# Writing out the last lap of an edge join and routing each 16 tiles inside it

## The reference, cut to what matters

```python
h = (x_flat @ W_gat).reshape(M, HEADS, NUM_EXPERTS)         # 4 heads, 4 experts
e = leaky_relu(a_src[src] + a_dst[dst], 0.2)                # each edge and head
ee = exp(e - segment_max(e, dst)[dst])
alpha = ee / (segment_sum(ee, dst)[dst] + 1e-16)
agg = segment_sum(h[src] * alpha[:, :, None], dst) + b_gat
scores = layernorm(agg, ln_gamma, ln_beta).reshape(M, HEADS, NUM_EXPERTS).mean(1)
topk_s, topk_i = top_k(scores, 2); w = softmax(topk_s)
out = sum over experts of gate * (gelu(x @ W1[e] + b1[e]) @ W2[e] + b2[e])
```

## Time and profile before

| what | us |
| --- | --- |
| median of 3 runs | 1663.26 (1662.75 to 1664.58) |
| profiled execution | 1661.68 |
| its span | 1659.9 |
| DVE busy | 1253.1 |
| PE busy | 873.8 |
| POOL busy | 868.6 |
| ACT busy | 444.9 |

### The profile page before, as it was taken

How to read it: one execution, slowest core, us unless ns; L and a number is a source line. 1 busy time by engine, 2 the same in 40 slices (tenths; PEclk the granted TensorE clock), 3 DMA queues, 4 the chain that set the end, 5 groups by cost and what they waited for, 6 DMA issues and landing times. The chain is left out here.

```text
span 1659.9 us, 37280 instructions
## 1 busy us (share of the span) xinstructions
PE 873.8 (53%) x13446; PEld 687.8 (41%) x13446; DVE 1253.1 (75%) x2683; ACT 444.9 (27%) x801; POOL 868.6 (52%) x892
## 2 busy tenths in 40 slices
PE   0232333268888825544888836656666556544300
PEld 0222233157777725542333325555555545444300
DVE  6989988866666647978999966677667667555599
ACT  0222222134444425751333312111111111111100
POOL 0045654646666630003777777760777777777200
PEclk9555555556767656765999965555555555555555
DMA  7000000122222234003110011100111111101001
GB/s 166 0 21 23 28 26 21 52 46 49 51 51 48 58 48 97 4 24 35 11 10 10 10 10 12 12 11 4 12 12 13 12 13 14 12 12 11 6 10 40
DMA packets 114003, 45.95 MB, mean 28 GB/s; under 512 B 92647, under 2 KB 108831, under 8 KB 113586
## 3 DMA queue, kind: packets, MB, share of 16 engines
q1 hardware_dynamic: 84098, 22.43, 7.1%
q0 software_dynamic: 27680, 19.22, 6.8%
q10 hardware_dynamic: 2064, 2.10, 0.6%
HBM read 28.26 MB, written 15.93 MB: 27 GB/s over the span
## 5 line engine op out<-in xcount | busy, mean ns | idle before, releaser
L335 POOL DMA_INDIRECT edges_rows<-table,edges_src x576 | 552.7, 960 | 175.6 <-issue 175.6
L191 DVE TENSOR_TENSOR sorting_keys<-sorting_keys 128x512 f32<-128x512 f32 (+2 forms) x370 | 209.7, 608 | 17.0 <-ACT sorting_keys L316 13.7
L727 POOL DMA_INDIRECT y_rows<-mixture_yt,mixture_xin x144 | 157.1, 1091 | 103.5 <-ACT mixture_yt L949 79.6
L722 POOL DMA_INDIRECT x_rows<-mixture_sent,mixture_slot x128 | 144.4, 1128 | 127.3 <-DVE mixture_slot L784 88.8
L2348 ACT ACTIVATE edges_hotT<-edges_h 128x1024 bf16<-128x1024 bf16 x74 | 71.7, 1021 | 391.4 <-PE edges_h L2247 391.4
L1062 PE MATMUL mixture_bank<-mixture_xT,sorting_w_part 128*128 128x128 bf16 x864 | 109.6, 254 | 32.4 <-ACT mixture_xT L935 17.2
L1062 PEld LDWEIGHTS mixture_bank<-mixture_xT,sorting_w_part 128*128 x864 | 85.3, 105 | 58.4 <-issue 46.4
L1897 DVE TENSOR_TENSOR edges_work<-edges_feats,all_eo 128x2048 bf16<-128x2048 f32 x48 | 109.3, 2277 | 0.2 <-DVE all_eo L1950 0.2
L2247 PE MATMUL edges_h<-edges_ident,edges_work 128*128 128x128 bf16 x592 | 68.7, 308 | 32.7 <-DVE edges_work L1897 32.7
L1897 DVE TENSOR_TENSOR edges_work<-edges_feats,edges_local 128x2048 bf16<-128x2048 f32 x37 | 84.4, 2282 | 0.3 <-DVE edges_stray_src L2053 0.3
L2301 PE MATMUL edges_acc<-edges_term_parts,edges_work 128*128 128x20 bf16 x1728 | 51.8, 179 | 60.5 <-DVE edges_term_parts L1776 60.5
(11 more groups left out here) (477 smaller groups left out, 2168.0 us busy)
## 6 DMA issues: line engine op xcount, KB each, us to landing
edges_rows<-table,edges_src POOLq DMA_INDIRECT x576, 2.4
mixture_xin<-x_rows SPq DMA_DIRECT2D x144, 49.0 KB, 1.8
all_eo<-y_rows SPq DMA_DIRECT2D x16, 256.0 KB, 3.9
y_rows<-mixture_yt,mixture_xin POOLq DMA_INDIRECT x144, 2.6
sorting_w<-in_L_ffn_w_dram SPq DMA_DIRECT2D x4, 512.0 KB, 8.4
x_rows<-mixture_sent,mixture_slot POOLq DMA_INDIRECT x128, 2.3
out_dram<-all_x_sb SPq DMA_DIRECT2D x8, 256.0 KB, 2.6
constants_src_i<-in_L_ffn_edge_index_dram SPq DMA_DIRECT2D x1, 1024.0 KB, 5.0
```

Of the source, the lines that this page charges most:

```text
L191: self.st.mark(dve.tensor_tensor(target[half], source[0], source[1], (ALU.min, ALU.max)[half]))
L335: pool.indirect_dma_start(to, None, rows, where).then_inc(done, 16)
L722: pool.indirect_dma_start(x_rows, bass.IndirectOffsetOnAxis(ap=slot[g % 2][:, c, t:t + 1], axis=0), now[c][:, t, :], None).then_inc(scatte ...
L727: pool.indirect_dma_start(y_rows, bass.IndirectOffsetOnAxis(ap=xin[j % XB][:, ROWX - 2:ROWX - 1].bitcast(U32), axis=0), yt[j % YB][:, :], ...
```

## The change

Four things are done together.
- **The last lap is written out** on every engine, and only the laps between the first and the last are a hardware loop (for this data one). In the last lap the order is group-major (`group_major`): the three turns of group 0, then those of group 1, and so on. POOL gathers in that order too. The floor of turns becomes seven.
- **Routing moves into the last lap.** When a group's three turns are done, its 16 tiles are routed during the three steps of the next group: `route_gaps` behind the first fetch of sums, `route_totals`, `route_scores` and `route_image` ahead of the wait for `now` in the first, second and third step, and the second half of the image work at the third step's end. The last group is routed behind the last step. The reduction over experts becomes two additions. The block `route` goes; its buffers are carved from the spent `stacks`, and its small loads are issued in `graph`. The mask `absent` is made ahead of the strays.
- **Keys are fetched further on**: POOL issues the key gather behind the last group of the second turn. DVE places sources of turns 0 and 1 in the 7th step of a lap, and those of turn 2 in the 9th, where it first waits for all gathers of the third turn. The last lap fetches no keys.
- **Fields, flags and the fetch of sums** are handled by lap: local numbers and flags of three turns are placed at once at a lap's end, and each step but a lap's first fetches the sums of the step before, also across turns. The last step of the last lap makes no next one-hots.

```diff
-        st.link(dve.tensor_scalar(self.most[:, :], self.most[:, :], float(LAP + 1), float(LAP - 1), ALU.max, ALU.add))
+        st.link(dve.tensor_scalar(self.most[:, :], self.most[:, :], float(2 * LAP + 1), float(LAP - 1), ALU.max, ALU.add))
-        st.link(dve.tensor_copy(self.laps[:, 0:1], self.thirds[:, :]))
+        st.link(dve.tensor_scalar(self.laps[:, 0:1], self.thirds[:, :], 1.0, None, ALU.subtract))
...
+        def turn_major(s):
+            return s // GROUPS % LAP, s % GROUPS
+
+        def group_major(s):
+            return s % LAP, s // LAP
...
-                        if u == 1 and g == 0 and not first:
-                            wait_apart(pool, at_ready, lap + 2, spare)
-                            gather(pool, krow[:, :], key_elements, at_i[0:T, :], keys_in)
+            for s in range(SEQ):
+                gather_group(0, *turn_major(s))
+            with pool.Fori(1, last_lap) as lap:
+                for s in range(SEQ):
+                    u, g = turn_major(s)
+                    gather_group(lap, u, g)
+                    if u == 1 and g == LAST:
+                        wait_apart(pool, at_ready, lap + 2, spare)
+                        gather(pool, krow[:, :], key_elements, at_i[0:T, :], keys_in)
+            for s in range(SEQ):
+                gather_group(last_lap, *group_major(s))
...
             dve.tensor_copy(times[:, :], times_ps).then_inc(times_read, 1)
+            dve.wait_ge(times_read, 1)
+            st.mark(dve.tensor_scalar(absent[:, :], times[:, :], 0.0, NONE, ALU.is_le, ALU.mult))
...
+            def route_gaps(q):
...
+                now = tiles(q)
+                rt.link(dve.tensor_tensor(shared, last_row[:, Q:ROW].unsqueeze(1).to_broadcast([P, TP, HEADS]), ad_sb[:, now, :], ALU.add))
+                rt.link(dve.scalar_tensor_tensor(shared, shared, 0.2, shared, ALU.mult, ALU.max))
+                rt.link(dve.tensor_tensor(shared, shared, per_channel(absent[:, now], HEADS), ALU.add))
+                rt.link(dve.tensor_tensor(top, tops[:, now, :], shared, ALU.max))
+                rt.mark(dve.tensor_tensor(gaps[:, 0, :, :], tops[:, now, :], top, ALU.subtract))
+                gaps_marks[q] = rt.n
+                dve.tensor_tensor(gaps[:, 1, :, :], shared, top, ALU.subtract).then_inc(gaps_ready, 1)
+
+            def route_totals(q):
...
+                dve.wait_ge(exps_ready, q + 1)
+                rt.mark(dve.tensor_tensor(by_head(total), by_head(sums[:, now, :]), wide(exps[:, 0, :, :], NE + 1), ALU.mult))
...
+                rt.link(dve.tensor_tensor(agg, agg, vector(0), ALU.add))
+                norm.center(dve, rt, agg, agg)
+
+            def route_scores(q):
...
+                norm.scale(dve, rt, agg, q, normed)
+                dve.wait_ge(normed, q + 1)
...
+                rank = order.unsqueeze(1).to_broadcast([P, TP, NE])
+                for n, values in enumerate((scores, others)):
+                    rt.link(dve.tensor_reduce(firsts[n], values, X, ALU.max))
+                    rt.link(dve.tensor_tensor(chosen, values, per_channel(firsts[n], NE), ALU.is_equal))
+                    rt.link(dve.tensor_tensor(chosen, chosen, rank, ALU.mult))
+                    rt.link(dve.tensor_reduce(best, chosen, X, ALU.max))
+                    rt.link(dve.tensor_tensor(masks[n], rank, per_channel(best, NE), ALU.is_equal))
...
+            def route_image(q, half=0):
...
+                rt.link(dve.tensor_tensor(weighted, eo[:, now, :].rearrange("p t (e c) -> p t e c", e=K),
+                                          gate[:, half * TB:(half + 1) * TB, :].unsqueeze(3).to_broadcast([P, TB, K, C]), ALU.mult))
+                rt.link(dve.tensor_tensor(added2, weighted[:, :, 0:2, :], weighted[:, :, 2:4, :], ALU.add))
+                rt.link(dve.tensor_tensor(x_sb[:, now, :], x_sb[:, now, :], added2[:, :, 0, :], ALU.add))
+                dve.tensor_tensor(x_sb[:, now, :], x_sb[:, now, :], added2[:, :, 1, :], ALU.add).then_inc(result, 1)
+                dve.wait_ge(result, b + 1)
+
+            def join_lap(lap, st, order_of, first=False, final=False):
...
-                        if g > 0:
-                            add_sums(u, g - 1)
...
+                        if s > 0:
+                            add_sums(s - 1)
+                        if final and s >= LAP and s % LAP == 0:
+                            route_gaps(done)
+                        if not first and not final:
+                            if s == GROUPS + LAST - 1:
+                                dve.wait_ge(keys_turned, lap + 2)
+                                place_sources(st, 0)
+                                place_sources(st, 1)
+                            if s == 2 * GROUPS:
+                                for n in range(GROUPS):
+                                    dve.wait_ge(rows_in[2][n], lap * (16 * GB) + 16 * GB)
+                                place_sources(st, 2)
+                        if first and s == SEQ - 1:
                             place_sources(st, 2)
-                            dve.wait_ge(flags_ready, lap * LAP + LAP)
+                        if s == SEQ - 1 and not final:
+                            dve.wait_ge(flags_ready, lap + 1)
                             keep_fields(st)
-                        if g == LAST:
-                            place_fields(st, (u + 1) % LAP)
+                            place_fields(st)
...
-                        one_hot(nxt)
+                        if not final or s < SEQ - 1:
+                            one_hot(s + 1, *order_of((s + 1) % SEQ))
...
                         st.mark(dve.tensor_copy(old, now[:, :]))
-                        dve.wait_ge(now_ready, at(u, g))
+                        if final and s >= LAP:
+                            (route_totals, route_scores, route_image)[s % LAP](done)
+                        dve.wait_ge(now_ready, at(s))
...
-                        if g == LAST:
-                            add_sums(u, g)
...
+                        if final and s >= LAP and s % LAP == LAP - 1:
+                            route_image(done, 1)
+                        if s == SEQ - 1:
+                            add_sums(s)
...
+            join_lap(last_lap, Steps(dve, final_steps), group_major, final=True)
+            route_gaps(GROUPS - 1)
+            route_totals(GROUPS - 1)
+            route_scores(GROUPS - 1)
+            route_image(GROUPS - 1)
+            route_image(GROUPS - 1, 1)
...
+            for s in range(SEQ):
+                done = s // LAP - 1
+                if done >= 0:
+                    if s % LAP == 0:
+                        route_exps(done)
+                    elif s % LAP == 1:
+                        norm.scalar(act, done)
+                    else:
+                        route_gate(done)
+                exp_group(turns * GROUPS + s, s, s < SEQ - 1)
```

More of the change, by code:

```diff
@@ L1 @@
 import itertools
+import math
 from contextlib import ExitStack
@@ L1640, in graph, with take @@
                               for n in range(2))
+        spent = [v[:, :].bitcast(F32) for v in stacks]
+        weighted = spent[0][:, 0:TB * K * C].rearrange("p (t e c) -> p t e c", t=TB, e=K)
+        added2 = spent[0][:, TB * K * C:TB * K * C + TB * 2 * C].rearrange("p (t e c) -> p t e c", t=TB, e=2)
+        vec = a.sb("vec", [P, 3, F])
+        last_row = a.sb("last_row", [P, ROW])
+        absent = a.sb("absent", [P, T])
+        used = 0
+        def take(*shape):
+            nonlocal used
+            words = math.prod(shape)
+            used += words
+            v = spent[1][:, used - words:used]
+            if len(shape) == 1:
+                return v
+            names = "abc"[:len(shape)]
+            return v.rearrange(f"p ({' '.join(names)}) -> p {' '.join(names)}", **dict(zip(names, shape)))
+        shared, top = take(TP, HEADS), take(TP, HEADS)
+        gaps, exps = take(2, TP, HEADS), take(2, TP, HEADS)
+        part3, total, inverse = take(TP, Q), take(TP, Q), take(TP, HEADS)
+        agg, scores, gate = take(TP, F), take(TP, NE), take(TP, NE)
+        order, chosen, others = take(NE), take(TP, NE), take(TP, NE)
+        best, gap2, gap2_exp = take(TP), take(TP), take(TP)
+        masks, firsts = [take(TP, NE) for _ in range(2)], [take(TP) for _ in range(2)]
+        shares = [take(TP) for _ in range(2)]
+        norm = Norm(a, "norm", TP, F, 1e-5, take(TP, F))
         carved = 0
```

360 lines of the change are left out of this document (161 added, 199 removed).

## The result

| | before | after |
|---|---|---|
| median (range) of the runs, us | 1663.44 (1662.75 to 1664.58) | 1599.07 (1597.70 to 1600.27) |
| span of the profiled execution, us | 1659.9 | 1598.4 |
| after / before | | 0.9612 [0.9595, 0.9629] |

The changed kernel is 3.9% faster; 1601 was forecast. Names of buffers and lines have moved with the change: the step's first instruction is L2219 now, the fetch of sums L2211, the gathers L336, the matmuls of `now` L2449, the routing pieces L2138 to L2199.

What follows compares the result with a forecast made beforehand. The prediction saw VectorE's chain of 36 steps, POOL's gathers beside it and a serial VectorE tail as bounds. 1513.1 + 56.0 + 28.8 = 1597.9 us of span, 62.0 less, so a median of 1601; range 1590 to 1617 (0.80).

Steps and rivals of the forecast that it cites:

- Key gather: On POOL, moved three groups later: reached at 1176.4 us with 21 us of margin, where 43.6 us of wait stood.
- POOL's end: POOL's gather stream: 19 groups of 20.07 us and one key gather after 1116.2, ending at 1498.8 us, against 1546.8.
- Start of the join: VectorE's first join step: 997.14 us plus 0.4 for the absent mask moved ahead of it.
- Laps 1 and 2: VectorE's first two laps of the join: 170.8 us, ending at 1168.3, then 175.5 us, ending at 1343.8.
- The term of the boundary: Fetching sums at each turn's end on VectorE: 2.3 us per boundary inside a lap, removed except at a lap's end.
- Last lap without routing: VectorE's written-out third lap: 13.1 + 10 x 14.1 + 15.2, together 169.3 us, ending at 1513.1.
- Routing in the lap: Three quarters on VectorE, 24.5 us each less 5.7 of cover in waits for PE: 56.0 us added.
- ScalarE: Six function table loads of 1.28 us in the last lap, costed at nothing; 7.7 us if not covered.
- (b): Rival: keys still come late, the 9th step of lap 2 waits 22 us for rows, 1623 us; chance 0.03.
- (a): Rival: routing in the lap is not covered; 17 us more gives 1618, up to 1628; chance 0.07 beyond 1617.
- (c): Rival: instruction fetch stalls the written-out last lap, slower than before, 1696 us with two refetches a step; chance 0.03.
- (d): Rival: the join does not shorten, late rows only change places with routing, 1653 us; chance 0.02.

Runs made afterwards that it cites:

- one-hot ahead: Version with both waits covered and the mask moved, plus 4 of 16 tiles of the next one-hot made before the fetch of sums; 1584.18 us, ratio 0.9537.

## Why the prediction was right, point by point

- **Key gather.** Near 1176 without a wait; it was at 1180.14. The move has its cause and price confirmed from both sides.
- **POOL's end.** Forecast 1498.8, measured 1514.5, the largest miss of a point. POOL reached the key gather 3.7 us late. The 256 gathers behind it take 333.1 us (1181.38 to 1514.51), 20.8 a group and not 20.07: they are 1.00 us long in the mean, four of them stretched by 7.1 us together (last section), while POOL waits for nothing but its own issue. The 20.07 was low by the earlier trace rows too, whose 552.7 and 175.6 us over 576 gathers make 20.23. It cost nothing with routing in the lap. But the forecast also held that POOL would be in time "even with no routing in the lap", and that was wrong: there the last gather was issued at 1505.45 and the last step came 6 us late. The forecast had set POOL's end against the end of the last step (1513.1), while a step wants its rows at its start, which by the same terms was 1497.9 and ahead of POOL's 1498.8.
- **Start of the join.** 1001.46, not 997.5. Of the 3.9, 2.2 already stand where `graph` loads its first constants, behind stages whose code is the same (748.18 became 750.34). The rest was counted as 0.4, and isn't split here. Part of it is spread between executions: two more traces with the code of the kernel before up to this point start the join at 998.62 and 998.84, where the earlier trace rows has 997.14.
- **Laps 1 and 2.** 172.2 and 175.1 us, where 170.8 and 175.5 were forecast. A plain step took 14.03, not the 13.93 of the earlier trace rows. The steps that place sources are 0.8 and 1.0 longer (1242.85, 1257.64, 1272.70), 0.6 was counted. **The term of the boundary was right in size and wrong in kind**: 2.3 is 1.3 of fetch and 1.0 of placing, and the placing wasn't removed but gathered at the lap's end, where the last step grew from 18.02 to 18.69.
- **The loop's end.** 3.94 us of idle time became 0.39. The kernel before with the moved keys still shows 3.51 there.
- **Last lap without routing.** 169.3 forecast; 13.0 + 10 x 14.03 + 14.34 = 167.6 by the trace with all routing behind it. The last step was the mis-sized term, 15.2 against 14.34; the plain steps, 14.1 against 14.03, add 0.7.
- **Routing in the lap.** 56.0 forecast, 54.1 measured. A quarter by itself is 24.98 with its 0.9 of waits for ScalarE, which the forecast counted apart: 24.05 without them against 24.5. The cover was 6.9 a quarter, 0.9 of it these waits and 6.0 the waits for TensorE, where 5.7 was counted. So the pieces were a little shorter and the cover a little wider than forecast. The place of the cover was right: the list of waits lost nine waits for `now`, and the piece behind the term's parts took the three at the sums.
- **Tail.** 28.8 forecast, 27.9 measured (1570.48 to 1598.4).
- **ScalarE.** Costed at nothing, and nothing is seen: decay, the first consumer behind a reload, is wanted at 1423.98 and was ready at 1420.79.

The span was 1597.9 by the sum and 1598.4 by the trace. That is closer than the steps are: 5.0 us too few up to the last lap, 3.6 too many in it and 0.9 too many in the tail. The mechanism held, but an agreement to half a microsecond is luck. Of the rivals, (b) is real with 15 us, 6 less than priced; (a) is what the kernel with all routing at the end does, 27 instead of 17 with the rows that come late; for (c) no idle time of issue above 0.39 us is seen at a step's start in the written-out lap; (d) fell, since the join's last sums come 5.5 us later than in the earlier trace rows with three quarters of the routing already in it.

## What to carry to other kernels

When a producer engine waits for an index, ask which step of the consumer releases it and move the wait, not the work: one condition was worth 32 us alone and 15 on top of the rest. Work moved from a tail onto the engine that is the bound gains only the waits that it fills; list them first, one by one, with the instruction that must stand ahead of each (here 1.5 and 1.2 us a step), and give both their piece. Before shortening what covers another engine's work, compare the cover's length with that work: from the point where they are equal the gain ends. And when a small edit moves the instructions of one engine against those of another, look for ones that have become longer before you look for waits: two edits here lost part of their gain in casts that took 0.24 and 0.44 us instead of 0.19 and 0.20.

## What the runs showed of the hardware

**Gathers are stretched while a product runs.** POOL's issue of one gather, 0.95 us, took 2.21, 2.85, 2.97 and 2.85 us at four places of the last lap. VectorE and POOL of the changed kernel at the first and second, each in order of time:

```profile
1437.43 2.29 DVE L2195 TENSOR_TENSOR all_stack<-all_eo,all_stack 128x2048 f32<-128x2048 f32 x1
...
1445.99 2.27 DVE L2195 TENSOR_TENSOR all_stack<-all_eo,all_stack 128x2048 f32<-128x2048 f32 x1
```

```profile
1438.33 2.21 POOL L336 DMA_INDIRECT edges_rows<-table,edges_src  x1 [0.30 <-issue]
...
1446.23 2.85 POOL L336 DMA_INDIRECT edges_rows<-table,edges_src  x1 [0.30 <-issue]
```

Both start under a product and end 0.8 us behind it. The stores of the lap are not the cause: with all of them behind the last image the same gathers take 2.20 and 2.85. The one-hots of 2.28 us, as long but with one input from PSUM, leave them alone: the 60 gathers that begin under one in the changed kernel's join take 0.94 or 0.95. Shorter instructions with two SBUF inputs do the same on their scale: 23 gathers begin under the subtraction of 128x320 in the term's parts (L1821, 0.49 us); they take 1.18 or 1.19 and end 0.81 to 0.83 behind it. The Trainium skill ("GPSIMD Engine Reference", Specifications) says that GpSimd shares its SBUF interfaces with VectorE, and names contention with instructions that run in a 2-port mode or have two SBUF inputs. The rows agree on the two inputs. That the second SBUF input is the cause is still argued from such comparisons; no kernel changed only where an input lies.

**A table switch costs its load.** ScalarE in the first quarter's steps:

```profile
1406.73 1.28 ACT L383 ACT_TABLE_LOAD   x1
1408.02 0.22 ACT L383 ACTIVATE edges_norm_root<-edges_norm_var 128x16 f32<-128x16 f32 x1
1417.28 1.94 ACT L2508 ACTIVATE edges_hotT<-edges_h 128x1024 bf16<-128x1024 bf16 x2 [9.04 <-PE edges_h L2403]
1419.23 1.28 ACT L2522 ACT_TABLE_LOAD   x1
1420.53 0.26 ACT L2522 ACTIVATE edges_decay<-edges_fall 128x64 f32<-128x64 f32 x1
```

From a load's start to the next activation it is 1.29 and 1.30 us, and the load starts at once behind the activation ahead of it. Nine idle microseconds follow the first switch. The Trainium skill ("ScalarE: Activation LUTs", What ACT_TABLE_LOAD costs) reckons with some 2.66 us for a switch and its drain; no drain shows in these rows. VectorE has no wait for ScalarE in the last lap of the changed kernel, so the page's rule to batch by function set would have gained nothing there.

**A gather stretches casts in turn, and so the plain step has several lengths.** For the same instructions it is 13.93 us in the kernel before and 14.03 in the changed one; with sums at the turn's end it is 13.92 in one profiled execution and 14.03 in the other. Granted clock is 0.50 in all of them at that place. What differs in the lines is, in the main, casts. In a step of 13.92 one of the three casts of the term's parts takes 0.40 us and the other two 0.33; in one of 14.03 two casts of the parts of `now` also take 0.29 and 0.22 where they took 0.20 and 0.19. With the key gather in its old place POOL stands still for 41.9 us; there no cast is stretched, and two steps take 13.85 and 13.83.

The pattern is the same in four traces (before, changed, keys back in their old place, one-hot ahead). Of the casts of 64 elements from SBUF, 155 took over 0.26 us. Each of them began 0.24 to 0.43 us before the end of a gather's issue and ended 0.00 to 0.03 behind that end, as in the step shown for the one-hot ahead. The 57 that began over 1 us behind the last gather took 0.18 to 0.20. The 315 that began earlier under a gather took 0.18 to 0.23. So the issue of a row gather, 0.94 us, holds up a cast that begins in its last 0.43 us, and none that begins before that. (One cast that began 0.39 us before the end of a key gather took 0.19; that gather fetches 64 rows and not 128.) What decides how gathers and casts fall against each other in an execution stays open. Over 30 steps the two lengths differ by 3 us, as much as the smallest effects above.
